# A scratch fill behind each gather on GpSimd, with one wait more for each pair of gathers

## The chip, the cores and the metric

The kernel runs on one core of a Trainium2 chip. The metric is device time in microseconds (us), the median of the timed runs. Engines are called by the profile's names: PE is TensorE (PEld its weight loads), DVE is VectorE, ACT is ScalarE, POOL is GpSimd, SP is SyncE. All of them run programs of their own and meet only at semaphores.

## The reference

A graph of 6250 nodes and 100000 edges goes through a two-layer attention network and then through a node update. What the change touches is the attention of each layer:

```python
scores = jnp.einsum('ehd,ehd->eh', q[dst], k[src]) * scale
m = jax.ops.segment_max(scores, dst, num_segments=n)
ex = jnp.exp(scores - m[dst])
z = jax.ops.segment_sum(ex, dst, num_segments=n)
attn = ex / z[dst]
agg = jax.ops.segment_sum(attn[:, :, None] * v[src], dst, num_segments=n)
```

Here n = 6250, there are 8 heads of 32 columns, and all is float32. Edges are sorted by dst, so q[dst] and the sums over dst work on nearby rows, while k[src] and v[src] are rows at random places.

## The kernel before

The program is a row of phases: tables and masks, an input projection, and then for each of two layers a projection to q, k and v (`project`), the attention (`attend`) and a feed-forward update (`update`), with `finish` at the end. Between phases all engines meet at a barrier.

`attend` handles 55 periods (NBA) for each layer. A period holds 16 units (UB) of 128 edges each, in four quarters q = 0 to 3 of four units. For each unit POOL issues one indirect DMA, a gather: it reads 128 rows of 2 KB (k and v side by side, `kv_scratch`) at the indices in `src_u` and writes them to one slot of the tile `kv`, which has room for three periods (RING). On the other engines, in one period:

- PE spreads the rows of q to the edges with one-hot matrices (`spread`, matmuls at L1296, signal `q_s`) and sums messages per node (`sum_up`, L1308, signal `sum_s`). The sums are those of edges gathered two periods earlier.
- DVE multiplies q by k (`products`, L1148, after a wait for the quarter's gathers), reduces to scores (L1155), weights v (`messages`, L1163), adds PE's sums to the table (`add`, L1174, after a wait for `sum_s`), and once in a period works through the running maximum (`chain_runs`).
- ACT makes the one-hot matrices (L1061, L1064, L1073, L1077) and the exponentials.
- SP loads the small tables of the next period.

Nothing is scheduled by a planner: each engine runs the order in which its code is written. POOL's part is the loop over pairs j = 0 to 7 of a period. Ahead of a pair stand its waits: for even j the messages of the slot that is overwritten (`msg_s`) and a query signal of PE (`q_s`), for odd j a sum signal of PE (`sum_s`), and for every j that the gathers of three pairs before (FLIGHT) have landed (`ring_in`). PE's signals that are waited for are those of one period earlier, so POOL runs at most one period ahead. `g.sem_inc(pool_go, 1)` is an instruction that carries the waits; nobody waits for `pool_go`.

Of the kernel before, what the change touches and what calls it, by code (L numbers as in the profile page):

```python
# [22 lines left out]
P = 128  # L23
# [21 lines left out]
UB = 2 * GB  # L45
# [46 lines left out]
def gnn_kernel(nc, x, src_tiles, dst_tiles, src_rows, src_cols, edge_attr, vor_v, cent_v,  # L92
# [28 lines left out]
    def sb(where, name, shape, dt=f32):  # L121
        return where.enter_context(nc.sbuf_tensor(f"{name}_{phase[0]}", shape, dt))
# [10 lines left out]
    with ctx:  # L133
# [14 lines left out]
        with ExitStack() as ph:  # L148
# [33 lines left out]
            s = Names(pool)  # L182
# [163 lines left out]
        with ExitStack() as ph:  # L346
# [9 lines left out]
            s = Names(pool)  # L356
# [537 lines left out]
        def attend(l):  # L894
# [9 lines left out]
            with ExitStack() as ph:  # L904
# [19 lines left out]
                right = sb(ph, "right", [P, BK + 1])  # L924
                edges_t = sb(ph, "edges_t", [P, 3, BK])
                own_block = sb(ph, "own_block", [P, H])
                cols = sb(ph, "cols", [P, 8])
                begin, not_first, unit_f, neg_p = cols[:, 0:3], cols[:, 3:6], cols[:, 6:7], cols[:, 7:8]
                top = sb(ph, "top", [P, BK // UB])
# [8 lines left out]
                s = Names(pool)  # L938
# [11 lines left out]

                scT_s, shift_s, chain_s = s.many(3)
                exp_s, wT_s, w_s, scale_s, rescaled = s.many(5)
                final_s, final_exp = s.many(2)
                CK = 16
                last_mask, in_run, out_run = slice(RW + 2 * P, MW), slice(RW, RW + P), slice(RW + P, RW + 2 * P)
                DVE_E, PE_E = mybir.EngineType.DVE, mybir.EngineType.PE
# [1 line left out]
                def wait(eng, sem, v):  # L958

                    if not isinstance(v, int) or v > 0:  # L960
                        eng.wait_ge(sem, v)

                def periods(eng, period, first, last):

                    for n in range(first, TURN):
                        period(n, n % 2, n // 2, n % RING)
                    with eng.Fori(1, NBA // TURN) as t:
                        for b in range(TURN):
                            period(t * TURN + b, b % 2, t * (TURN // 2) + b // 2, b % RING)
                    for n in range(NBA // TURN * TURN, last + 1):  # L970
                        period(n, n % 2, n // 2, n % RING)
# [10 lines left out]
                with nc.Block() as block:  # L982
# [40 lines left out]
                    @block.gpsimd  # L1023
                    def _(g):
                        g.iota(unit_i[:, 0:1], [[0, 1]], base=0, channel_multiplier=1).then_inc(consts, 1)

                        def period(n, par, t, ring):
                            g.wait_ge(src_in[par], t * 16 + 16)
                            for j in range(GB):
                                if j % 2 == 0:  # L1030
                                    wait(g, msg_s, n * GQ - RING * GQ + j // 2 + 1)
                                    wait(g, q_s, n * GQ - GQ + j // 2 + 2)
                                else:
                                    wait(g, sum_s, n * GQ - RING * GQ + j // 2 + 1)
                                if j >= FLIGHT:
                                    g.wait_ge(ring_in[par * GB + j - FLIGHT], t * 32 + done[par] + 32)
                                elif not isinstance(n, int) or n > 0:
                                    g.wait_ge(ring_in[(1 - par) * GB + GB + j - FLIGHT], (t + par) * 32 + done[1 - par])
                                g.sem_inc(pool_go, 1)
                                for u in (2 * j, 2 * j + 1):  # L1040
                                    slot = ring * UB + u
                                    g.indirect_dma_start(  # L1042
                                        out=kv[:, slot, :], out_offset=None, in_=KVd,
                                        in_offset=bass.IndirectOffsetOnAxis(ap=src_u[:, par, u:u + 1], axis=0),
                                        bounds_check=NPA - 1, oob_is_err=False).then_inc(ring_in[par * GB + j], 16)

                        periods(g, period, 0, NBA - 1)
                        for pair in range(2 * GB):
                            g.wait_ge(ring_in[pair], done[pair // GB] + 32 * rounds[pair // GB])
# [991 lines left out]
        late.close()  # L2041
        project(0)
        attend(0)
        with ExitStack() as keeping:
            held = sb(keeping, "held", [P, NT * HELD, YW])
            held_dest = sb(keeping, "held_dest", [P, NT * HELD], i32)
            update(0, held, held_dest)
            project(1, held, held_dest)
        attend(1)
        update(1)  # L2050
        finish()
# [40 lines left out]
```

## Time and profile before

| | |
|---|---|
| timed runs, median of 3 | 4550.55 us (4545.4 to 4551.32) |
| profiled execution, its span on the chip | 4968.2 us |
| POOL, DVE, PE busy in that span | 3293.4, 3674.6, 3781.3 us |
| gathers (L1042) | 1760, mean 1009 ns, 1775.7 us |
| adds of PE's sums (L1174) | 880, 433.7 us, idle before them 463.9 us |

The profiled execution has no time of its own beside its span; it is a separate execution from the three timed ones. A row of a view gives for a group of instructions its busy time and how long its engine was idle before it, with what ended that idle time; "issue" is idle time for which the profile shows no waiting, and "remote" is a release whose sender the profile doesn't know. The ends of PE's matmuls are modelled.

### The profile page before, as it was taken

How to read it: one execution, taken by the hardware profiler on the slowest of the kernel's cores; microseconds unless marked ns; L12 is line 12 of the kernel's file. 1: busy time of each engine (PE TensorE's matmuls, PEld its weight loads, DVE VectorE, ACT ScalarE, POOL GpSimd, SP SyncE). 2: the span in 40 equal slices, each digit the busy share in tenths (PEclk: the TensorE clock that was granted, in tenths of full speed). 3: DMA queues.
4: the chain of work that ended last, by engine and by line, in shares of the span. 5: the costliest groups of instructions: out<-in, count | busy, mean ns of one | idle time of the engine just before them, and what ended most of it. 6: DMA issues, size and time to landing. Idle time of an engine off the chain costs nothing. (4 is left out here: it accounts for less than half of the span.)

```text
span 4968.2 us, 83663 instructions
## 1 busy us (share of the span) xinstructions
PE 3781.3 (76%) x17490; PEld 2898.5 (58%) x17491; DVE 3674.6 (74%) x10004; ACT 2245.8 (45%) x5559; POOL 3293.4 (66%) x2856
## 2 busy tenths in 40 slices
PE   2686677777777776999986677777777776888879
PEld 1344455555555555888853455555555555777766
DVE  5686688888888886666656688888888886666658
ACT  0122455555555553444410455555555563343323
POOL 2266666666666654888877666666666663888866
PEclk9698799988988998999998799999899997999989
DMA  4577666666666655777766666666666654777767
GB/s 107 176 173 172 195 184 180 184 181 180 185 175 184 178 159 127 152 160 153 160 133 132 199 181 187 183 181 181 180 180 181 183 172 97 148 143 148 143 157 222
DMA packets 683884, 831.82 MB, mean 167 GB/s; under 512 B 147301, under 2 KB 524321, under 8 KB 683589
## 3 DMA queue, kind: packets, MB, share of 16 engines
q0 software_dynamic: 261248, 480.06, 40.8%
q1 hardware_dynamic: 389483, 320.59, 22.4%
q10 hardware_dynamic: 32860, 28.05, 1.9%
q8 instruction: 88, 1.44, 0.1%
q14 instruction: 205, 1.68, 0.1%
HBM read 753.81 MB, written 124.16 MB: 177 GB/s over the span
## 5 line engine op out<-in xcount | busy, mean ns | idle before, releaser
L1042 POOL DMA_INDIRECT kv<-kv_scratch,src_u x1760 | 1775.7, 1009 | 955.1 <-issue 532.4
L1308 PE MATMUL sum_p<-msg,hot_s 128*128 128x273 f32 x3520 | 1132.7, 460 | 578.9 <-DVE sums L1174 452.6
L1308 PEld LDWEIGHTS sum_p<-msg,hot_s 128*128 128x128 f32 x3520 | 705.2, 215 | 893.1 <-DVE sums L1174 442.8
L1523 POOL DMA_INDIRECT sum_scratch<-ysum,dest x600 | 951.8, 1586 | 196.8 <-issue 137.8
L1296 PE MATMUL qe<-sums,hot_q 128*128 x3520 | 910.0, 404 | 99.6 <-ACT hot_q L1064 85.7
L1296 PEld LDWEIGHTS qe<-sums,hot_q 128*128 128x128 f32 x3520 | 719.5, 208 | 244.7 <-issue 115.7
L1174 DVE SCALAR_TENSOR_TENSOR sums<-sums,keep,sum_p 128x273 f32 x880 | 433.7, 493 | 463.9 <-remote 402.1
L1073 ACT ACTIVATE hot_s<-iota_f,ndrel_u 128x128 f32<-128x128 f32 x1760 | 558.7, 391 | 223.1 <-remote 173.2
L1148 DVE TENSOR_TENSOR prod<-qe,kv 128x1024 f32<-128x1024 f32 x440 | 535.6, 1217 | 64.2 <-DMA kv<-kv_scratch,src_u 35.0
L1163 DVE TENSOR_TENSOR msg<-kv,turned 128x1024 f32<-128x1024 f32 x440 | 532.6, 1210 | 7.5 <-issue 7.5
L1155 DVE TENSOR_REDUCE S<-prod 128x32 f32<-128x1024 f32 x440 | 533.8, 1213 | 0.6
L1061 ACT ACTIVATE hot_q<-drow,cols 128x512 f32<-128x512 bf16 x440 | 312.3, 710 | 264.6 <-DMA kv_scratch<-zero 125.0
L1809 PE MATMUL w_p<-xT,w_s 128*128 128x128 f32 x3200 | 375.9, 276 | 1.3 <-ACT xT L1714 0.7
L1809 PEld LDWEIGHTS w_p<-xT,w_s 128*128 128x128 f32 x3200 | 365.2, 192 | 2.9 <-issue 1.8
L1819 PE MATMUL w_p<-w_s,uT 128*128 128x256 f32 x1600 | 361.9, 379 | 0.0
L1734 ACT ACTIVATE ysum<-y_p 128x396 f32<-128x396 f32 x200 | 100.3, 501 | 521.9 <-PE y_p L1766 496.7
L1064 ACT ACTIVATE hot_q<-hot_q,ones 128x512 f32<-128x512 f32 x440 | 317.7, 722 | 14.3
L1077 ACT ACTIVATE hot_s<-hot_s,ones 128x512 f32<-128x512 f32 x440 | 317.6, 722 | 14.3
L1819 PEld LDWEIGHTS w_p<-w_s,uT 128*128 128x128 f32 x1600 | 296.2, 190 | 36.1
L1722 ACT ACTIVATE uT<-w_p,b_c 128x128 f32<-128x128 f32 x800 | 228.9, 369 | 142.8 <-PE w_p L1809 104.5
L859 PE MATMUL mma<-w,xT 128*128 128x512 f32 (+1 forms) x600 | 270.7, 580 | 4.6 <-issue 1.1
L578 ACT ACTIVATE xT<-tp 128x256 f32<-128x256 f32 x156 | 59.8, 384 | 438.7 <-PE tp L852 375.2
(267 smaller groups left out, 5147.8 us busy)
## 6 DMA issues: line engine op xcount, KB each, us to landing
drow<-drel_scratch SPq DMA_DIRECT2D x220, 256.0 KB
kv<-kv_scratch,src_u POOLq DMA_INDIRECT x1760
ea<-in_edge_attr SPq DMA_DIRECT2D x52, 512.0 KB
srow<-in_src_rows SPq DMA_DIRECT2D x52, 512.0 KB
kv_scratch<-res SPq DMA_DIRECT2D x100, 256.0 KB
ea<-in_edge_attr SPq DMA_DIRECT2D x52, 384.0 KB
srow<-in_src_rows SPq DMA_DIRECT2D x52, 384.0 KB
h_scratch<-res SPq DMA_DIRECT2D x150, 128.0 KB
```

The source lines that it names most:

```text
L1042: g.indirect_dma_start(out=kv[:, slot, :], out_offset=None, in_=KVd, in_offset=bass.IndirectOffsetOnAxis(ap=src_u[:, par, u:u + 1], axis=0 ...
L1064: a.activation(hot, hot, ACT.Relu, bias=ones[:, 0:1], scale=-1.0).then_inc(hot_q_s, 1)
L1073: ins = a.activation(hot_s[:, q % 2, u, :], iota_f[:, :], ACT.Abs, bias=ndrel_u[:, par, q * 4 + u:q * 4 + u + 1])
L1148: v.tensor_tensor(out=prod[:, :, :], in0=qe[q % 2][:, :, :].rearrange("p b (u d) -> p (b u) d", d=D), in1=kv[:, ring * UB + 4 * q:ring * U ...
L1155: v.tensor_reduce(out=S[:, par, :, 4 * q:4 * q + 4].rearrange("p h u -> p u h"), in_=heads(prod[:, :, :]), axis=AX.X, op=ALU.add).then_inc ...
L1163: v.tensor_tensor(out=heads(msg[:, q % 2, :, 0:D]), in0=heads(kv[:, slot:slot + 4, D:2 * D]), in1=turned[par][:, 0:P].rearrange("p (r u) - ...
L1174: v.scalar_tensor_tensor(out=at, in0=at, scalar=keep[:, bass.ds(c, 1)], in1=sum_p[i][:, 0:XW], op0=ALU.mult, op1=ALU.add).then_inc(add_s, 1)
L1296: ins = pe.matmul(qe[q % 2][:, i, u * D:(u + 1) * D], hot_q[:, q % 2, 2 * i + u, :], sums[:, bass.ds(tile * XW + XW, D)], start=True, stop ...
L1308: ins = pe.matmul(sum_p[i][:, 0:XW], hot_s[:, q % 2, 2 * i + u, :], msg[:, q % 2, 2 * i + u, :], start=(u == 0), stop=(u == 1))
L1523: g.indirect_dma_start(out=sum_d[r], out_offset=bass.IndirectOffsetOnAxis(ap=dest[:, k, j:j + 1], axis=0), in_=ysum[:, k, j, :], in_offset ...
L1809: ins = pe.matmul(w1_p[f][:, b * P:(b + 1) * P], w1_s[:, c, j * P:(j + 1) * P], xT[:, k, c * P:(c + 1) * P], start=(c == 0), stop=(c == 1))
L1819: pe.matmul(w2_p[:, k * D:(k + 1) * D], uT[:, k, j, :], w2_s[:, j, :], start=(j == 0), stop=False)
```

## The change

Behind each gather POOL fills 128 columns of one of two halves of a scratch tile `pause` with zeros (a MEMSET of 128 partitions by 128 columns of float32), which counts up a new semaphore, `pause_s`. Ahead of each pair of gathers, behind the waits that were there already, POOL waits until all fills so far are done. Nobody reads the tile. All other waits stay.

```diff
@@ -924,6 +924,7 @@
                 own_block = sb(ph, "own_block", [P, H])
+                pause = sb(ph, "pause", [P, 2, P])
                 cols = sb(ph, "cols", [P, 8])
@@ -950,7 +951,7 @@
-                final_s, final_exp = s.many(2)
+                final_s, final_exp, pause_s = s.many(3)
@@ -1036,6 +1037,7 @@
                                 elif not isinstance(n, int) or n > 0:
                                     g.wait_ge(ring_in[(1 - par) * GB + GB + j - FLIGHT], (t + par) * 32 + done[1 - par])
+                                wait(g, pause_s, n * UB + 2 * j)
                                 g.sem_inc(pool_go, 1)
@@ -1043,6 +1045,7 @@
                                         bounds_check=NPA - 1, oob_is_err=False).then_inc(ring_in[par * GB + j], 16)
+                                    g.memset(pause[:, u % 2, :], 0.0).then_inc(pause_s, 1)
```

On POOL, in the middle of a layer, the order of before is two gathers for each set of waits; sem19 is `msg_s`, sem16 is `q_s`, sem21 is `sum_s`:

```order
L1042 DMA kv<-kv_scratch,src_u 128x512 [waits ring_in3,sem19,sem16]
L1042 DMA kv<-kv_scratch,src_u 128x512
L1042 DMA kv<-kv_scratch,src_u 128x512 [waits sem21,ring_in4]
L1042 DMA kv<-kv_scratch,src_u 128x512
L1042 DMA kv<-kv_scratch,src_u 128x512 [waits ring_in5,sem16,sem5,sem19]
```

The same two pairs in the changed kernel, on POOL; sem33 is `pause_s`:

```order
L1044 DMA kv<-kv_scratch,src_u 128x512 [waits sem33,ring_in3,sem19,sem16]
L1048 MEMSET pause 128x128
L1044 DMA kv<-kv_scratch,src_u 128x512
L1048 MEMSET pause 128x128
L1044 DMA kv<-kv_scratch,src_u 128x512 [waits sem33,sem21,ring_in4]
L1048 MEMSET pause 128x128
L1044 DMA kv<-kv_scratch,src_u 128x512
L1048 MEMSET pause 128x128
```

No gather has moved against another. A fill stands behind each, and the first gather of every pair now also waits for the fill just ahead of it. The order on the other engines is as before.

## Rows read from the trace of the kernel before

**Rows 1.** Windows inside both attention stages: busy time and count by engine.

```profile
core 0: us, PE busy (x) PEld busy (x) DVE busy (x) ACT busy (x) POOL busy (x), PEclk, DMA share, GB/s
744.00:868.00 124.00, 95.03 (x367) 70.70 (x368) 103.62 (x192) 74.14 (x177) 81.31 (x81) 0.92 0.63 183
992.00:1116.00 124.00, 94.39 (x361) 70.53 (x360) 102.18 (x189) 72.18 (x171) 80.02 (x80) 0.89 0.62 182
3100.00:3224.00 124.00, 93.97 (x365) 69.68 (x365) 102.28 (x190) 72.34 (x174) 82.12 (x82) 0.92 0.63 185
```

**Rows 2.** Timeline of POOL, half a period: start, duration, idle before and releaser.

```profile
1007.05 1.01 POOL L1042 DMA_INDIRECT kv<-kv_scratch,src_u  x1 [0.30 <-issue]
1008.37 1.01 POOL L1042 DMA_INDIRECT kv<-kv_scratch,src_u  x1 [0.30 <-issue]
1009.68 1.01 POOL L1042 DMA_INDIRECT kv<-kv_scratch,src_u  x1 [0.30 <-issue]
1012.91 1.00 POOL L1042 DMA_INDIRECT kv<-kv_scratch,src_u  x1 [2.23 <-remote]
```

**Rows 3.** Timeline of the other engines in the same stretch.

```profile
1005.99 2.01 PE L1308 MATMUL sum_p<-msg,hot_s 128*128 128x273 f32 x8
...
1007.47 1.21 DVE L1163 TENSOR_TENSOR msg<-kv,turned 128x1024 f32<-128x1024 f32 x1
...
1012.11 0.99 ACT L1073 ACTIVATE hot_s<-iota_f,ndrel_u 128x128 f32<-128x128 f32 x3 [1.92 <-remote]
1012.27 0.50 DVE L1174 SCALAR_TENSOR_TENSOR sums<-sums,keep,sum_p 128x273 f32 x1 [3.60 <-remote]
```

**Rows 4.** The adds (L1174), layer 0 and layer 1: idle before them (us, times).

```profile
L1174 DVE SCALAR_TENSOR_TENSOR sums<-sums,keep,sum_p x440: 481/491/502, 556.0 to 1892.2; 128x273 f32 x147
...
  remote: 198.6, 66
...
L1174 DVE SCALAR_TENSOR_TENSOR sums<-sums,keep,sum_p x440: 485/491/502, 2804.8 to 4139.2; 128x273 f32 x147
...
  remote: 203.5, 67
```

**Rows 5.** Gathers (L1042), by layer: ns min/median/max, first and last start.

```profile
L1042 POOL DMA_INDIRECT kv<-kv_scratch,src_u x880: 1000/1007/1303, 483.9 to 1846.1; - x176
...
L1042 POOL DMA_INDIRECT kv<-kv_scratch,src_u x880: 1001/1007/1305, 2732.4 to 4093.8; - x176
```

**Rows 6.** Fills of this shape, and POOL's other work behind and ahead of indirect DMAs.

```profile
L1498 POOL MEMSET tril<- 128x128 f32 x2 | 0.4, 206 | 110.4 <-POOLq L130 110.4
...
2207.39 1.54 POOL L1523 DMA_INDIRECT sum_scratch<-ysum,dest  x1 [0.31 <-issue]
2208.40 1.14 POOL L1505 TENSOR_TENSOR rs<-veps,columns 128x1 f32<-128x1 f32 x1
2209.73 1.72 POOL L1523 DMA_INDIRECT sum_scratch<-ysum,dest  x1 [0.19 <-issue]
2211.75 1.54 POOL L1523 DMA_INDIRECT sum_scratch<-ysum,dest  x1 [0.30 <-issue]
...
L665 POOL TENSOR_TENSOR rs<-veps,columns 128x1 f32<-128x1 f32 x52 | 28.7, 552 | 138.4 <-DVE veps L710 138.4
```

**Rows 7.** The instruction (L1039) that holds POOL's waits, near 1012 us.

```profile
L1039 POOLq EVENT_SEMAPHORE  x1: 43/43/43, 1012.1 to 1012.1; - x1
```

**Rows 8.** Products (L1148), by layer, and POOL's first gathers of layer 0.

```profile
L1148 DVE TENSOR_TENSOR prod<-qe,kv x220: 1210/1217/1225, 494.1 to 1860.0; 128x1024 f32<-128x1024 f32 x110
...
L1148 DVE TENSOR_TENSOR prod<-qe,kv x220: 1212/1217/1226, 2741.4 to 4107.1; 128x1024 f32<-128x1024 f32 x110
...
487.96 1.01 POOL L1042 DMA_INDIRECT kv<-kv_scratch,src_u  x1 [0.31 <-issue]
```

## Prediction

> **What bounds the kernel now.** I read the busy time by windows first, because the change touches the two attention stages alone. There, 124 us hold 80 to 82 POOL instructions, all of them gathers [rows 1]: 16 gathers, one period, take about 24.8 us. DVE is the busiest engine, with 102 to 104 of 124 us, so about 20.6 us of the period; POOL has 80 to 82 us. Neither is full, so I went to the timeline of one half period. POOL's gathers follow each other at 1.31 us (1.01 of work and 0.30 of launch), and then there is a hole of 2.23 us [rows 2]. If there were no holes, 16 gathers would take 21.0 us. DVE has a hole too: its message multiply ends at 1008.68, and the add behind it starts at 1012.27, 3.60 us later [rows 3]. That add waits for a sum signal of PE. The sum matmuls are modelled to end at 1008.00 [rows 3], 4 us before ACT, DVE and POOL, which all wait for that signal, go on together at 1012.1 to 1012.9 [rows 2, 3]. So PE's signal reaches everyone late, and it is what POOL's hole and DVE's hole have in common. The adds show what it costs: DVE sat idle before them, with an unknown sender, for 198.6 us in layer 0 and 203.5 us in layer 1 [rows 4], together 402 us, or 3.7 us in each of 110 periods. Without it a period would be about 24.8 - 3.7 = 21.1 us, which is at once POOL's 21.0 and little over DVE's 20.6.
>
> The span is 4968.2 us and the median of the timed runs 4550.55, which is 417.65 us less. That is very near the 402 us of late signals. I take this as the likeliest reading: in the executions that are timed, the signals aren't late, or hardly, and attention runs there at about 21 us a period, with POOL already full. No row proves it; the other reading, that the signals are as late in the timed runs and that the difference lies elsewhere, is a rival.
>
> **What the change adds on POOL.** Nothing is removed, and no instruction of another engine changes. There are 1760 fills and 880 waits, one for each pair. I add up one pair, from the moment at which the wait for the fills ends to the same moment of the next pair.
>
> - *Restart.* The wait stands ahead of the pair, and it can end only when the second fill of the pair before is done. In the profile before, the sequencer prepares a gather while the last one runs, and that is why the launch costs just 0.30 us. After a real wait it does not: the instruction with the waits goes at 1012.1 [rows 7], ACT starts on the same signal at 1012.11 [rows 3], and the gather starts at 1012.91 [rows 2], 0.80 us on. With 0.05 for the instruction itself [rows 7] I take 0.85.
> - *First gather:* 1.00, as after the hole [rows 2].
> - *First fill.* A fill of this very shape takes 206 ns [rows 6]. A POOL operation behind an indirect DMA: the DMA ends at 2208.93, the operation, 0.55 us long by itself, at 2209.54, so 0.61 later [rows 6]. It costs its own duration and 0.06. For the fill that makes 0.26.
> - *Second gather.* It starts 0.19 after the operation [rows 6]. The DMA behind an operation took 1.72 in place of 1.54 [rows 6]; I take half of that difference, so 0.19 + 1.10.
> - *Second fill:* 0.26.
>
> The sum is 0.85 + 1.00 + 0.26 + 0.19 + 1.10 + 0.26 = 3.66 us for a pair, against 2.62 for a pair without holes and 3.10 as the profile has it now (24.8 / 8). A period takes 8 x 3.66 = 29.3 us. That is more than the 24.8 of the trace, late signals included, and much more than DVE's 20.6: POOL becomes the bound, and everything that waits for gathers goes at its pace.
>
> Bounds of the pair. Below, the fill could fit wholly into the 0.30 us of launch: 0.80 + 1.00 + 0.30 + 1.00 + 0.21 = 3.31. Above, a fill may start later than its neighbour did, say by another 0.10 each, and the gather behind it take the full 0.18 more: 0.85 + 1.00 + 0.36 + 0.19 + 1.19 + 0.36 = 3.95. I take 3.66 because all its terms stand in rows of the same engine with the same neighbours.
>
> The Trainium skill, GPSIMD Engine Reference, section 2.1, says that consecutive Pool instructions are no barrier between the eight cores: a core begins the next instruction as soon as its own share is done, and only completion on all cores releases a semaphore wait. The trace agrees in so far as the small operation is shown from 2208.40 on, inside the DMA that ends at 2208.93 [rows 6]. By that rule the first fill could cost next to nothing, but the wait for the second could not be dodged; the pair would be near the lower bound of 3.31.
>
> **What goes away.** If the late signals have to do with gathers that follow each other closely, they may vanish, because gathers now start 1.45 and 2.2 us apart. That gains nothing: POOL's own 29.3 us is longer than the period with the late signals. The waits for messages, queries, sums and landed gathers don't add anything either. PE's signals are those of the period before, and DVE, which trails POOL by a landing, has some 24 us of slack for them. What is late next is the landing of a quarter's gathers, which DVE meets at the products (L1148).
>
> **The sum.** A layer has 440 pairs: 440 x 3.66 = 1610 us. From the fourth gather's end (487.96 + 1.01) to the first product at 494.1 there are 5.1 us [rows 8], and so the last product comes about 1615 us after the first gather. Before, it came 1860.0 - 483.9 = 1376.1 and 4107.1 - 2732.4 = 1374.7 us after it [rows 5, 8]. That is +239 and +240 us; what follows the last product stays. The profiled execution goes to 4968.2 + 479 = 5447 us. Here the readings of the 417.65 us part. Since POOL's pace doesn't depend on PE's signals, the timed runs lose what they had over the profile, all but 417.65 - 402 = 16 us: 5447 - 16 = **5431, say 5430 us**. Seen from the timed runs it is the same: 110 periods from 21.1 to 29.3 us.
>
> With the pair at 3.31 the layer takes 1461 us, +86 and +87, and the timed run 4968 + 173 - 16 = 5125. With 3.95 it takes 1743, +367 and +368, so 5687.
>
> **The rivals.**
>
> *The signals are late in the timed runs too*, and the profile is longer for other reasons. Then the timed run gains only the difference seen in the trace: 4550 + 479 = 5029 us. For it: the trace is the only witness, and it shows the signals late. Against: 402 and 417.65 are hardly equal by chance. I give it 0.27.
>
> *The restart is not paid.* If the wait is answered while the sequencer is still ahead, a pair is 2 x 1.31 and two fills of 0.25, so 3.12 us, 25.0 us a period. That is the 24.8 of the trace and 3.9 over 21.1: 4550 in the one reading, 4550 + 110 x 3.9 = 4980 in the other. Against: the wait is for the very fill that runs last. 0.07, and 0.03 more for a fill that costs nothing at all (2.62 us, no change).
>
> *Faster.* The late signals are real in the timed runs, the spaced gathers end them, and the pair stays below 3.10 us, from which point on POOL is quicker than the period of now. With fills hidden in the launch and no restart, say 2.84 us a pair, POOL's period is 22.7 us, 2.1 less: 4550 - 110 x 2.1 = 4319. For it: the hole always follows a run of gathers at 1.31 us. Against: it needs three things at once, and the restart of 0.80 alone lifts the pair over 3.10. 0.05.
>
> *The fill waits longer*, for example the full 0.61 of its neighbour: 0.85 + 1.00 + 0.61 + 0.19 + 1.19 + 0.61 = 4.45 us, 35.6 a period, 1958 us a layer, +583 each: 4968 + 1166 - 16 = 6118. Against: the neighbour takes 0.55 by itself and the fill 0.21. 0.06.
>
> **How the numbers follow.** The forecast has 0.52, and within it I expect 5125 to 5687, most of it between 5250 and 5580. The range reaches down to take in the first rival, with its 5029, and stops short of the far ends: 4990 to 5590. A measurement of this kernel tells a change of about 0.2% from none. Faster is 0.05, within that bound 0.03, slower 0.52 + 0.27 + 0.07 + 0.06 = 0.92.
>
> **What would show it.** In the profile after: gathers in pairs, the second 1.4 to 1.6 us after the first and the next pair over 2 us after that; POOL's group of fills with 1760 x about 0.2 to 0.3 us; idle time before the products that a landed gather ends, and little of the 402 us before the adds; a span of about 5447 us, with the timed median within 1% of it. If the span is about 5450 and the timed median near 5030, the pair was right and the reading of the 417.65 us was wrong. If the gap between pairs is 0.3 to 0.6 us, the restart was wrong. If DVE still waits at the adds, the late signals do not depend on the spacing of gathers.

## The result and the profile after

The changed kernel takes 5359.52 us (5357.33 to 5360.21, 4 runs), the kernel before 4549.89 us (4 runs). The ratio is 1.1785, with a 95% interval of 1.177 to 1.1799: 810 us or nearly 18% slower. The forecast was 5430.

This is the timeline of POOL in the changed kernel, a little over one pair, with start, duration, operation and the idle time before it:

```profile
1003.39 1.01 POOL L1044 DMA_INDIRECT kv<-kv_scratch,src_u  x1 [0.96 <-POOL pause L1048]
1004.40 0.22 POOL L1048 MEMSET pause<- 128x128 f32 x1
1004.79 1.01 POOL L1044 DMA_INDIRECT kv<-kv_scratch,src_u  x1 [0.17 <-issue]
1005.79 0.22 POOL L1048 MEMSET pause<- 128x128 f32 x1
1006.89 1.01 POOL L1044 DMA_INDIRECT kv<-kv_scratch,src_u  x1 [0.87 <-POOL pause L1048]
```

Where [rows 2] had gathers at 1.31 us and then a hole of 2.23 us, there is now a hole of 0.87 or 0.96 us ahead of every pair, with a fill named as what ended it. A fill begins when its gather ends, takes 0.22 us, and the next gather starts 0.17 us later. From 1003.39 to 1006.89 the pair takes 3.50 us.

The groups of POOL and DVE in the whole program of after, with busy time and mean, then idle time before them and its causes:

```profile
L1044 POOL DMA_INDIRECT kv<-kv_scratch,src_u x1760 | 1787.5, 1016 | 975.1 <-POOL pause L1048 702.5
L1151 DVE TENSOR_TENSOR prod<-qe,kv 128x1024 f32<-128x1024 f32 x440 | 537.8, 1222 | 887.4 <-DMA kv<-kv_scratch,src_u 650.9
L1177 DVE SCALAR_TENSOR_TENSOR sums<-sums,keep,sum_p 128x273 f32 x880 | 432.2, 491 | 28.2 <-PE sum_p L1311 21.8
L1048 POOL MEMSET pause<- 128x128 f32 x1760 | 388.1, 221 | 0.8
```

POOL waits 702.5 us for its own fills. DVE waits 887.4 us ahead of the products, most of it for gathers to land: POOL sets its pace. The idle time before the adds, 402 us of late signals in [rows 4], is 28.2 us in all.

One window inside each attention stage of after, with the columns of [rows 1]:

```profile
992.00:1116.00 124.00, 88.19 (x321) 64.82 (x320) 90.62 (x163) 65.17 (x157) 86.11 (x141) 0.88 0.56 158
3400.00:3524.00 124.00, 87.02 (x312) 64.07 (x311) 88.10 (x162) 62.52 (x148) 85.55 (x139) 0.87 0.57 159
```

DVE's busy time is down from 102 to some 90 us in 124 [rows 1], and the 141 POOL instructions are gathers and fills, so about 70 gathers: some 28 us for 16. (The trace behind [rows 1] turns out in the next section to be no good measure of before.)

### The profile page after: what moved, and what is told of

It is laid out like the page before. It is cut to its first block and busy times, and to the rows that moved or that the text cites. A ratio compares the mean times of both kernels' runs of the same rounds, so it can differ in the third digit from the quotient of the medians.

```text
span 5357.9 us, 86583 instructions
## 1 busy us (share of the span) xinstructions
PE 3905.8 (73%) x17490; PEld 2972.4 (55%) x17491; DVE 3686.9 (69%) x10004; ACT 2255.3 (42%) x5559; POOL 3690.9 (69%) x4616
## 5 line engine op out<-in xcount | busy, mean ns | idle before, releaser
L1044 POOL DMA_INDIRECT kv<-kv_scratch,src_u x1760 | 1787.5, 1016 | 975.1 <-POOL pause L1048 702.5
L1311 PE MATMUL sum_p<-msg,hot_s 128*128 128x273 f32 x3520 | 1149.1, 457 | 838.2 <-DVE sums L1177 837.4
L1311 PEld LDWEIGHTS sum_p<-msg,hot_s 128*128 128x128 f32 x3520 | 691.6, 213 | 1161.7 <-DVE sums L1177 980.9
L1151 DVE TENSOR_TENSOR prod<-qe,kv 128x1024 f32<-128x1024 f32 x440 | 537.8, 1222 | 887.4 <-DMA kv<-kv_scratch,src_u 650.9
L1299 PE MATMUL qe<-sums,hot_q 128*128 x3520 | 1037.8, 447 | 101.3 <-ACT hot_q L1067 62.8
L1299 PEld LDWEIGHTS qe<-sums,hot_q 128*128 128x128 f32 x3520 | 799.6, 231 | 283.5 <-issue 124.7
L1177 DVE SCALAR_TENSOR_TENSOR sums<-sums,keep,sum_p 128x273 f32 x880 | 432.2, 491 | 28.2 <-PE sum_p L1311 21.8
L1048 POOL MEMSET pause<- 128x128 f32 x1760 | 388.1, 221 | 0.8
L1095 ACT ACTIVATE scale<-turned 128x8 f32<-128x8 f32 x110 | 19.6, 178 | 767.1 <-PE turned L1340 767.1
```

The source lines that it names most:

```text
L1044: g.indirect_dma_start(out=kv[:, slot, :], out_offset=None, in_=KVd, in_offset=bass.IndirectOffsetOnAxis(ap=src_u[:, par, u:u + 1], axis=0 ...
L1048: g.memset(pause[:, u % 2, :], 0.0).then_inc(pause_s, 1)
L1151: v.tensor_tensor(out=prod[:, :, :], in0=qe[q % 2][:, :, :].rearrange("p b (u d) -> p (b u) d", d=D), in1=kv[:, ring * UB + 4 * q:ring * U ...
L1177: v.scalar_tensor_tensor(out=at, in0=at, scalar=keep[:, bass.ds(c, 1)], in1=sum_p[i][:, 0:XW], op0=ALU.mult, op1=ALU.add).then_inc(add_s, 1)
L1299: ins = pe.matmul(qe[q % 2][:, i, u * D:(u + 1) * D], hot_q[:, q % 2, 2 * i + u, :], sums[:, bass.ds(tile * XW + XW, D)], start=True, stop ...
L1311: ins = pe.matmul(sum_p[i][:, 0:XW], hot_s[:, q % 2, 2 * i + u, :], msg[:, q % 2, 2 * i + u, :], start=(u == 0), stop=(u == 1))
```

## Experiment 1: the kernel before, traced again

The profiled execution of before that the prediction read had a span of 4968.2 us and late signals of TensorE. The unchanged kernel was run and traced once more, with no edit.

> The kernel before, unchanged, for a second trace of it. The profile that the prediction read has a span of 4968.2 us and late TensorE signals, while the four experiments so far have spans within 0.1% of their timed executions. The theory: that one execution was not like the timed ones; a new trace has a span near 4545 us, idle time before the adds under 60 us, and periods of about 21 us. Rival, tracing this kernel always makes its TensorE signals late: the span is again near 4968 us, with some 400 us idle before the adds.

It took 4548.25 us (ratio 0.9998, interval 0.9988 to 1.0009), and the traced execution's span is 4554.5 us. POOL in its timeline:

```profile
1003.77 1.01 POOL L1042 DMA_INDIRECT kv<-kv_scratch,src_u  x1 [0.30 <-issue]
1005.08 1.01 POOL L1042 DMA_INDIRECT kv<-kv_scratch,src_u  x1 [0.30 <-issue]
1006.40 1.01 POOL L1042 DMA_INDIRECT kv<-kv_scratch,src_u  x1 [0.30 <-DMA kv<-kv_scratch,src_u]
1007.71 1.01 POOL L1042 DMA_INDIRECT kv<-kv_scratch,src_u  x1 [0.30 <-DMA kv<-kv_scratch,src_u]
```

The groups of its gathers, adds and products, with busy time and mean, then idle time before them:

```profile
L1042 POOL DMA_INDIRECT kv<-kv_scratch,src_u x1760 | 1779.9, 1011 | 556.3 <-issue 356.8
...
L1174 DVE SCALAR_TENSOR_TENSOR sums<-sums,keep,sum_p 128x273 f32 x880 | 432.2, 491 | 32.8 <-PE sum_p L1308 28.1 <-issue 0.2
...
L1148 DVE TENSOR_TENSOR prod<-qe,kv 128x1024 f32<-128x1024 f32 x440 | 535.9, 1218 | 99.6 <-DMA kv<-kv_scratch,src_u 80.3 <-issue 12.3 <-PE qe L1296 6.2
```

And the window that answers to the second of [rows 1]:

```profile
992.00:1116.00 124.00, 103.53 (x433) 76.71 (x431) 119.09 (x226) 83.93 (x206) 94.58 (x94) 0.97 0.71 213
```

The holes of [rows 2] and [rows 3] aren't there, and the adds wait 32.8 us in all. DVE is busy 119 of 124 us, and 94 gathers fit where [rows 1] had 80: 16 gathers take 21.1 us. This is the profile of before with which the change has to be compared. DVE is the busiest engine, at 96%, but POOL sets the pace. Of the 556.3 us that POOL is idle before its gathers, 1760 x 0.30 = 528 us are the launches, so that it stops for hardly anything else, and 16 x 1.31 = 21.0 us is the whole period. DVE is the one that waits, 80.3 us for gathers to land. The median distance from a gather to the one a period later is 21.07 us. The measured pair goes from 2.63 us (21.07 / 8) to 3.50 or a little more.

The first and last starts give the layers. In the changed kernel, gathers of layer 0 and products of both:

```profile
L1044 POOL DMA_INDIRECT kv<-kv_scratch,src_u x880: 1011/1012/1277, 484.8 to 2055.2; - x176
...
L1151 DVE TENSOR_TENSOR prod<-qe,kv x220: 1208/1224/1226, 495.0 to 2057.4; 128x1024 f32<-128x1024 f32 x110
...
L1151 DVE TENSOR_TENSOR prod<-qe,kv x220: 1210/1224/1226, 2941.9 to 4505.3; 128x1024 f32<-128x1024 f32 x110
```

In the kernel before, as traced again:

```profile
L1148 DVE TENSOR_TENSOR prod<-qe,kv x220: 1210/1217/1226, 495.2 to 1655.7; 128x1024 f32<-128x1024 f32 x110
...
L1148 DVE TENSOR_TENSOR prod<-qe,kv x220: 1210/1217/1226, 2537.8 to 3698.4; 128x1024 f32<-128x1024 f32 x110
```

First to last product took 1160.5 and 1160.6 us before, and takes 1562.4 and 1563.4 us now: +402 and +403, together 805 of the 810 us. POOL's 440 pairs of layer 0 take (2055.2 - 484.8) / 440 = 3.57 us each.

## Experiments 2 to 10

Theory: the price is the restart. A wait for an instruction that is still to finish on the same engine stops POOL's sequencer from preparing the next gather, and each such wait costs 0.87 - 0.17 = 0.70 us. The fills add what they take beyond the launch that they share. The 0.70 us was read from the trace of after; the runs below test it. Rivals: the fills are the price; or TensorE's signals, late or waited for, have a part in it.

**Fills kept, the wait asks for older fills.** Pair j now waits for the fills up to the end of pair j - 2.

```diff
-                pause = sb(ph, "pause", [P, 2, P])
+                pause = sb(ph, "pause", [P, 4, P])
-                                wait(g, pause_s, n * UB + 2 * j)
+                                wait(g, pause_s, n * UB + 2 * j - 2)
-                                    g.memset(pause[:, u % 2, :], 0.0).then_inc(pause_s, 1)
+                                    g.memset(pause[:, u % 4, :], 0.0).then_inc(pause_s, 1)
```

> The fills stay, but the wait asks only for the fills up to the pair before last's end plus one (two fills less), on a tile of four slots, so that it is answered before POOL asks. The theory: the costly part of the change is the restart behind the wait, 0.87 us of the 3.50 us that a pair takes in the changed kernel's trace, in place of 0.17 us. A pair is then 2 x (1.01 + 0.22 + 0.17) = 2.80 us against 2.62 before; if POOL is the bound of the timed runs before, that is 880 x 0.18 = +158 us, 4710 us. Rival 1, the fills themselves cost: the time stays near 5300. Rival 2, POOL has slack in the timed runs before: 4550 to 4600. In the profile: if TensorE's late signals depend on gathers that follow each other at 1.31 us, they are gone at 1.40 us and the span is near the timed median; if not, the span is some 400 us over it and the idle time before the adds stays near 400 us.

4682.74 us, ratio 1.0305 (1.0288 to 1.0322), span 4683.3 us. That is 139 us over its own runs of before (4543.34). The same 1760 fills, and 670 of the 810 us are gone. POOL's timeline:

```profile
1003.28 1.01 POOL L1044 DMA_INDIRECT kv<-kv_scratch,src_u  x1 [0.17 <-issue]
1004.28 0.23 POOL L1048 MEMSET pause<- 128x128 f32 x1
1004.67 1.01 POOL L1044 DMA_INDIRECT kv<-kv_scratch,src_u  x1 [0.16 <-POOL pause L1048]
1005.69 0.22 POOL L1048 MEMSET pause<- 128x128 f32 x1
1006.07 1.01 POOL L1044 DMA_INDIRECT kv<-kv_scratch,src_u  x1 [0.17 <-issue]
```

A pair takes 2.79 us with no hole. The wait is still there, in front of the gather at 1004.67, and costs nothing, because what it asks for was done one pair earlier. Nearly all of the last 139 us is a period that grows from 21.07 to 8 x 2.79 = 22.3 us, 110 times.

What the wait does to the sequencer can be read in both traces. POOLq is POOL's sequencer; L1041 carries the waits, and one MOVE of L1044 belongs to each gather. The lines give durations in ns, then the first and last start in us. The changed kernel, from 1006 to 1007 us:

```profile
L1041 POOLq EVENT_SEMAPHORE  x1: 17/17/17, 1006.1 to 1006.1; - x1
L1044 POOLq MOVE  x2: 29/29/29, 1006.1 to 1006.7; - x2
```

And the version of this experiment, from 1003 to 1006.5 us:

```profile
L1041 POOLq EVENT_SEMAPHORE  x1: 17/17/17, 1004.5 to 1004.5; - x1
L1044 POOLq MOVE  x2: 29/29/29, 1004.6 to 1005.2; - x2
```

In the changed kernel the fill ends at 1006.02, the waits and the first MOVE follow at 1006.1, and the gather starts at 1006.89. Counted off in order, the MOVE of a pair's first gather never comes before the last fill has ended, and it ends 0.73 us (median) ahead of its gather. In the version here the sequencer also waits for a fill, the one that ends at 1004.51, but its MOVE at 1004.6 is for the gather at 1007.47, and it is 2.7 us ahead in the median. So the sequencer may wait, as long as it waits ahead of the engine; what the change costs is that the wait takes this lead away.

**The wait kept, hardly any fill.** One column behind the second gather of a pair.

```diff
-                                wait(g, pause_s, n * UB + 2 * j)
+                                wait(g, pause_s, n * GB + j)
-                                    g.memset(pause[:, u % 2, :], 0.0).then_inc(pause_s, 1)
+                                g.memset(pause[:, 0, 0:1], 0.0).then_inc(pause_s, 1)
```

> One fill of a single column behind the second gather of each pair, and the wait for it ahead of the next pair. The theory: a pair is 1.01 + 0.30 + 1.01 + 0.10 + 0.87 = 3.29 us, so 880 x (3.29 - 2.62) = +590 us on 4550, 5140 us, nearly three quarters of the change's cost with a fill of almost nothing. Rival, the fills are what costs and the wait is cheap: 4550 to 4650 us.

5179.48 us, ratio 1.14 (1.138 to 1.1419). Its timeline on POOL:

```profile
1001.52 1.00 POOL L1044 DMA_INDIRECT kv<-kv_scratch,src_u  x1 [0.87 <-POOL pause L1048]
1002.83 1.00 POOL L1044 DMA_INDIRECT kv<-kv_scratch,src_u  x1 [0.30 <-issue]
1003.83 0.12 POOL L1048 MEMSET pause<- 128x1 f32 x1
1004.82 1.00 POOL L1044 DMA_INDIRECT kv<-kv_scratch,src_u  x1 [0.87 <-POOL pause L1048]
```

The hole is 0.87 us again behind a fill of 0.12 us, and the time rises by 636 us against the 4543.34 of its own runs of before. So the hole doesn't depend on how long the fill is.

**The wait ahead of every other pair, and ahead of every gather.** Both have all fills of 128 columns.

```diff
-                                wait(g, pause_s, n * UB + 2 * j)
+                                if j % 2 == 0:
+                                    wait(g, pause_s, n * UB + 2 * j)
```

(with four slots of the tile, as above)

> The changed kernel with all fills, but the wait for them ahead of even pairs alone (a tile of four slots). The theory, a fixed price for each blocking wait: 440 waits fewer of 0.70 us each than in the changed kernel, so 5360 - 880 x 0.70 / 2 = 5052 us, or from the version with lagged waits 4683 + 308 = 4991 us; 4990 to 5050. Rival, POOL makes up for a restart as long as one remains in each period, or DVE's slack swallows it: under 4900 us.

```diff
                                 for u in (2 * j, 2 * j + 1):
+                                    if u % 2 == 1:
+                                        wait(g, pause_s, n * UB + u)
+                                        g.sem_inc(pool_go, 1)
```

> The changed kernel with the wait for all fills ahead of the second gather of each pair as well. The theory, a fixed price of 0.70 us for each blocking wait on POOL's path: a pair is 2 x (1.01 + 0.22 + 0.87) = 4.20 us in place of 3.50, so 5360 + 880 x 0.70 = 5975 us. Rival, one restart in a pair already covers what the second would cost: under 5500 us.

5033.27 us (ratio 1.1066, 1.1047 to 1.1084) and 6005.32 us (1.3205, 1.3181 to 1.3229). With the lagged version and the change itself that makes four points: no blocking wait 4683, 440 waits 5033, 880 waits 5360, 1760 waits 6005. With each run taken against its own runs of before, the steps are 0.79, 0.74 and 0.73 us a wait. The 0.70 us seen in the timeline is most of each. The rest is in part waits behind which POOL restarted a little later: in the changed kernel the 781 holes that a fill ended come to 702.5 us, 0.90 each and not 0.87. A row of the version with a wait for every gather shows one:

```profile
1004.17 1.01 POOL L1047 DMA_INDIRECT kv<-kv_scratch,src_u  x1 [0.99 <-PE qe L1302]
```

The price of one wait hardly depends on how many there are: POOL does not make up for a restart, and slack of DVE does not swallow it.

**The size of the fill, without a blocking wait.** 16 and 512 columns in place of 128 in the lagged version.

```diff
-                                    g.memset(pause[:, u % 4, :], 0.0).then_inc(pause_s, 1)
+                                    g.memset(pause[:, u % 4, 0:16], 0.0).then_inc(pause_s, 1)
```

> The version with lagged waits, its fills cut from 128 to 16 columns. A fill of one column took 0.11 us, one of 128 took 0.22, so 16 columns are some 0.12; with the 0.17 us of launch behind it that is the 0.30 us which the launch takes without a fill. The theory: a pair is 2.60 to 2.62 us again and the fills are free: within 0.3% of the kernel before, 4548 us. Rival, each fill has a fixed price of 0.09 us on top of the launch: 4683 us stays.

```diff
-                pause = sb(ph, "pause", [P, 4, P])
+                pause = sb(ph, "pause", [P, 4, 4 * P])
```

> The version with lagged waits, its fills widened from 128 to 512 columns. POOL's fill of 13923 columns took 11.7 us, 0.84 ns a column, so 512 columns are 0.22 + 0.32 = 0.54 us and a pair is 2 x (1.01 + 0.54 + 0.17) = 3.44 us. The theory, POOL's gathers and fills are strictly one after the other: 4683 + 880 x 0.64 = 5246 us, close to the change itself with its 3.50 us, though nothing waits. Rival, long fills overlap the gathers because the descriptors are made by a part of GpSimd alone: under 5000 us.

4559.78 us (ratio 1.0025, 1.0014 to 1.0037) and 5242.88 us (1.1524, 1.1502 to 1.1547). One gather and fill of each, first 16 and then 512 columns:

```profile
1001.88 0.13 POOL L1048 MEMSET pause<- 128x16 f32 x1
1002.19 1.01 POOL L1044 DMA_INDIRECT kv<-kv_scratch,src_u  x1 [0.18 <-issue]
```

```profile
1001.05 0.54 POOL L1048 MEMSET pause<- 128x512 f32 x1
1001.75 1.01 POOL L1044 DMA_INDIRECT kv<-kv_scratch,src_u  x1 [0.16 <-POOL pause L1048]
```

A launch without a fill takes 0.30 us, one with a fill 0.17 beyond the fill. So 0.13 us of fill are free, and what lies beyond is paid: 0.09 us for 128 columns, 0.41 for 512 by the timelines, 0.08 (139 / 1760) and 0.39 (693 / 1760) by the medians. No overlap of long fills with gathers shows. The 10 us that are left with the small fill fit its gathers at 1.32 us (0.31 between two of them) in place of 1.31.

**Without POOL's waits for TensorE.** The same edit on the kernel before and on the changed one:

```diff
-                                    wait(g, q_s, n * GQ - GQ + j // 2 + 2)
-                                else:
-                                    wait(g, sum_s, n * GQ - RING * GQ + j // 2 + 1)
```

> The kernel before without POOL's waits for the query and sum signals (the waits for messages, landed gathers and indices stay, so that POOL may run up to two periods ahead). The theory: in the timed runs before, these waits are met when POOL asks, and the median stays within 0.5% of 4550. Rival, POOL is held by late TensorE signals in the timed runs too: the median falls by 2% or more, because POOL no longer waits for them. In the profile: longer unbroken runs of gathers; if that is what makes the signals late, the idle time before the adds grows over 400 us and the span over 4968 us.

> The changed kernel without POOL's waits for the query and sum signals. The theory: with fills and the wait for them POOL itself is the bound, and TensorE's signals hold it only for the some 50 us that its trace shows as idle before gathers by PE's qe and sum_p; the median stays within 1% of 5360, at most 50 us less. Rival, part of the change's cost is that POOL, once slower, meets those waits late: the median falls by more than 100 us.

4546.8 us on the kernel before (ratio 1.0013, 1.0003 to 1.0022) and 5342.69 us on the changed one (1.1758, 1.1739 to 1.1778, where the change itself has 1.1785). POOL's waits for TensorE's signals cost the kernel before nothing. In the changed one they cost little: 17 us by the medians, 12 by the ratios, whose intervals overlap.

**Half the bytes.** On the kernel before, with the same 1760 gathers:

```diff
-                                        out=kv[:, slot, :], out_offset=None, in_=KVd,
+                                        out=kv[:, slot, 0:D], out_offset=None,
+                                        in_=KVd.rearrange("n (c d) -> (n c) d", c=2),
```

(and `messages` reads the same half; v is left out and other rows are read, so that only the time says something)

> The kernel before, but each gather fetches 1 KB in place of 2 KB for each row (k alone, and the wrong row of it), and the messages are made of that half: the number and the pace of the gathers stay, the bytes in flight are halved. If TensorE's late signals come from bytes in flight, they are gone: idle time before the adds under 100 us, and a profile span within 1% of the timed median. If they come from the pace of POOL's gathers, the span stays near 4950 us with some 400 us of idle time before the adds. The timed median is near 4550 in both, if POOL's 2.62 us a pair is the bound there; if the late signals also cost time in the timed runs and come from the bytes, it falls by up to 400 us.

4530.23 us, ratio 0.9968 (0.9954 to 0.9981), span 4533.9 us. The bytes are worth 0.3%. The run was meant to tell where the late signals come from; but they are gone in the unchanged kernel's second trace too, so it tells nothing on that.

## Why the prediction was right

- *What bounds the kernel.* The forecast took the 402 us of late signals [rows 4] for a thing of the one profiled execution and put the timed period at 21.1 us. The second trace has 21.07. It named POOL as already full, and POOL it is: it stops for hardly more than its launches, and 0.09 us more for each gather lengthened the kernel by 139 us. DVE stands close behind, busy for 119 of 124 us.
- *The pair*, term by term, forecast and measured: restart 0.85 and 0.87, first gather 1.00 and 1.01, first fill 0.26 and 0.22, launch 0.19 and 0.17, second gather 1.10 and 1.01, second fill 0.26 and 0.22. The sum was 3.66, against 3.50 in the timeline and 3.57 over layer 0. The restart carried the price, and its mechanism was right from a few rows [rows 2, 3, 7]: the sequencer's lead is gone, and 0.73 us lie between its MOVE and the gather. The terms taken from the neighbour in [rows 6] were too large: a fill behind a gather adds nothing to its own 0.22 us, and the gather behind a fill isn't longer. Against the timeline the sum is 0.16 us too large, and 0.07 of that came back by luck: POOL's idle time before its gathers is 975.1 / 880 = 1.11 us for a pair, against 0.87 + 0.17 = 1.04 in the timeline, because some restarts take longer and 20 of the second gathers start 1.4 us behind their fill, for a reason that stays open. What is left, 0.09 us over 880 pairs, is 79 us; the forecast was 70 us too high.
- *The waits for TensorE.* The forecast put them at nothing. Without them the changed kernel is 12 to 17 us faster, which is not clear of noise.
- *The reading of the 417.65 us* was right: the changed kernel's traced span is 5357.9 us beside a median of 5359.52. The rival with late signals in the timed runs gave 5029 and is out. The span rose by just 390 us over the first trace, the timed median by 810.
- *The other rivals.* "The restart is not paid" is what the lagged wait does on purpose, and it came to 4683 rather than 4980, because its fills were costed at 0.25 us on top of the whole launch. "Faster" needed late signals in the timed runs; there were none to remove, as the second trace shows. The low idle time before the adds was to tell whether spaced gathers end the late signals; it can't, since the second trace of before has it too, with a gather every 1.31 us.
- *The Trainium skill*, GPSIMD Engine Reference, section 2.1: the completion of a Pool instruction holds back whatever waits for its semaphore, not the next Pool instruction. The trace agrees on the wait, which is passed at 1006.1, just behind the fill's end at 1006.02. But of the overlap that the rule allows, the trace shows none for a fill: it starts when the gather's row ends (1004.40), and 512 columns cost their whole length but 0.13 us.

What stays open is why TensorE's signals came late in the first profiled execution. Nothing here brought them back: ten traces, of before again and of variants of both kernels, of which four run gathers at 1.30 to 1.32 us, have spans within some 10 us of their timed medians.

## What to carry to other kernels

On POOL, ahead of an indirect DMA, a wait for its own last instruction costs the engine's restart, and that price doesn't depend on the length of the instruction: here 0.76 us for each of 880 waits, 670 of the 810 us. If a scratch tile needs such a wait, give it more slots (here four in place of two) and wait for the uses of one pair earlier, so that the sequencer stays ahead. Other engines were not tried. And where the span of a profile is far from the timed median, look for the idle time that makes the difference, and trace again before you build on it.

## What was not expected of the hardware

A fill behind an indirect DMA is free up to 0.13 us, since the launch behind it shrinks from 0.30 to 0.17 us. And one execution of an unchanged kernel can differ by 414 us in span (4968.2 and 4554.5), nearly all of it in waits for one engine's signals (the 402 us before the adds), at the same work: 83663 instructions and nearly the same busy time of DVE (3674.6 and 3661.1 us).
